# CIN tower: VectorE half a chunk behind TensorE, layer 0's K-tiles in the slots where pairs close, the first small product on VectorE

## What is computed

```python
e = stack([tbl_f[ids[:, f]] for f in range(32)], axis=1)     # 512 x 32 fields x 32
def cin(x0, filters):                                        # two layers, fp32
    prev, outs = x0, []
    for W in filters:                                        # (1, 32*32, 128), (1, 32*128, 128)
        z = einsum('bhd,bmd->bhmd', x0, prev).reshape(b, h * m, d)
        prev = relu(einsum('bpd,pn->bnd', z, W[0]))
        outs.append(prev)
    return sum(concatenate(outs, axis=1), axis=-1)
h = concatenate([cin(e, (filter_0, filter_1)), dense_ctx], axis=1)
y = relu(relu(h @ W_top1 + b_top1) @ W_top2 + b_top2) @ W_top3
```

## Time and profile before

| | |
|---|---|
| median of the runs | 988.39 us (988.18 to 989.77, 3 runs) |
| the profiled execution | 989.2 us, its span 987.4 us |
| TensorE busy | 872.2 us (88%), 3444 matmuls |
| VectorE busy | 770.8 us (78%) |
| ScalarE busy | 646.3 us (65%) |
| GpSimd busy | 682.4 us (69%) |
| granted TensorE clock, mean | 0.988 |

### The profile page before, as it was taken

The page is one execution under the profiler, slowest core; times in us unless marked ns, Lnnn a source line. Parts: engine busy times, 40 slices in busy tenths (PEclk is TensorE's granted clock), DMA queues, the critical chain, the costliest instruction groups (busy, mean ns, idle before and its releaser), DMA issues.

```text
span 987.4 us, 13153 instructions
## 1 busy us (share of the span) xinstructions
PE 872.2 (88%) x3444; PEld 646.5 (65%) x3444; DVE 770.8 (78%) x2506; ACT 646.3 (65%) x2174; POOL 682.4 (69%) x460
## 2 busy tenths in 40 slices
PE   0328999999999999999999999999999999999967
PEld 0105777776777777776777777776777777777743
DVE  0112888987888888898888888888888888888892
ACT  1208776777776777677777677777777767776702
POOL 6776887776787778777787777665666666666610
PEclk9998999999999999999999999999999999999988
DMA  9043221212222222212122222212111112110000
GB/s 255 14 147 114 73 72 59 62 60 72 72 72 72 72 73 72 64 59 67 62 72 73 73 72 72 71 59 87 47 50 70 70 69 70 70 59 1 1 1 0
DMA packets 34670, 66.64 MB, mean 67 GB/s; under 512 B 6226, under 2 KB 19762, under 8 KB 30403
## 3 DMA queue, kind: packets, MB, share of 16 engines
q1 hardware_dynamic: 27570, 59.94, 17.7%
q0 software_dynamic: 4096, 2.11, 1.8%
q10 hardware_dynamic: 2928, 3.76, 1.3%
HBM read 62.64 MB, written 5.24 MB: 69 GB/s over the span
## 4 chain that ended last, share of the span: by engine, by line
PE 66%; DVE 24%; POOL 5%; issue 3%; ACT 1%; DMA 0%; POOLq 0%
DVE acc L503 12%; PE acc L578 11%; PE yd L560 10%; PE yd L562 9%; PE yd L561 9%; PE ya L560 8%; PE ya L562 8%; PE ya L561 8%; POOL emb L260 5%; DVE yd L512 5%; DVE prev_lo L474 2%; DVE yd L503 2%; DVE sum L485 2%; DVE sum L518 1%; ACT scaled L399 1%
## 5 line engine op out<-in xcount | busy, mean ns | idle before, releaser
L399 ACT ACTIVATE scaled<-ya,emb 128x128 f32<-128x128 f32 x2048 | 584.2, 371 | 236.9 <-PE ya L562 234.7
L503 DVE SCALAR_TENSOR_TENSOR acc<-yd,emb,acc 128x128 f32<-128x128 f32 x1792 | 484.9, 341 | 105.1 <-PE yd L562 105.1
L279 POOL TENSOR_TENSOR half<-scaled 128x1024 f32<-128x1024 f32 x128 | 306.3, 2393 | 206.2 <-ACT scaled L399 205.1
L560 PE MATMUL yd<-w_hi,prev_hi 128*128 128x512 f32 x512 | 242.1, 473 | 44.1 <-DVE sum L518 43.3
L560 PE MATMUL ya<-w_hi,prev_hi 128*128 128x512 f32 x512 | 202.4, 395 | 3.5 <-ACT scaled L399 1.8
L561 PE MATMUL yd<-w_lo,prev_hi 128*128 128x512 f32 x512 | 202.1, 395 | 0.0
L562 PE MATMUL yd<-w_hi,prev_lo 128*128 128x512 f32 x512 | 201.9, 394 | 0.0
L561 PE MATMUL ya<-w_lo,prev_hi 128*128 128x512 f32 x512 | 200.9, 392 | 0.0
L562 PE MATMUL ya<-w_hi,prev_lo 128*128 128x512 f32 x512 | 200.9, 392 | 0.0
L283 POOL TENSOR_TENSOR part<-half 128x512 f32<-128x512 f32 x128 | 165.1, 1290 | 18.1 <-POOL half L279 0.4
L560 PEld LDWEIGHTS yd<-w_hi,prev_hi 128*128 128x128 f32 x512 | 97.1, 190 | 103.0 <-DVE sum L518 63.6
(11 more groups left out here) (52 smaller groups left out, 365.8 us busy)
## 6 DMA issues: line engine op xcount, KB each, us to landing
xb<-xt_scratch SPq DMA_DIRECT2D x32, 1024.0 KB, 5.0
x<-xt_scratch SPq DMA_DIRECT2D x64, 192.0 KB
xm<-xt_scratch SPq DMA_DIRECT2D x32, 256.0 KB, 4.8
emb<-in_tbl,idx POOLq DMA_INDIRECT x128, 2.5
scaled<-in_L_rec_filter SPq DMA_DIRECT2D x8, 256.0 KB, 6.1
xt_scratch<-xt_stage SPq DMA_DIRECT2D x7, 256.0 KB
xt_scratch<-xt_stage SPq DMA_DIRECT2D x9, 128.0 KB, 1.9
w_second_index_twice<-in_L_rec_filter ACTq DMA_DIRECT2D x2, 512.0 KB, 6.0
```

Source lines behind the costliest of these rows:

```text
L279: pool.tensor_tensor(half[:], piece[:, 0:AB * C // 2], piece[:, AB * C // 2:AB * C], ALU.add).then_inc(halved, 1)
L399: op = act.activation(scaled[:, tile % PR, C * j + N * i:C * j + N * (i + 1)], ya[:, n % RA, N * i:N * (i + 1)], ACT.Copy, scale=scale_of( ...
L503: dve.scalar_tensor_tensor(after, y_part, scale_of(c, q, HB * j + i), before, ALU.mult, ALU.add).then_inc(chained, 1)
L560: pe.matmul(dst, v_hi, m_hi, start=start, stop=False)
```

## The change

- D banks trail by half a chunk: slots 0 to 3 hold pair 1 of chunk c-1, slots 4 to 7 pair 0 of chunk c itself. The last round has four slots.
- K-tiles: slots 2 and 3 hold K-tiles 2 and 3 of chunk c+1 and the rest, slots 6 and 7 K-tiles 0 and 1 of chunk c+2. VectorE's products stand in slots 0 and 1 and in 5 and 6. `whole` has three buffers (`WH`).
- prev_high, prev_low and the addition to sum0 move to slot 4, copy_xm to slot 2, small_high (of chunk c+2) to slot 7; on GpSimd small_product (of chunk c+2) stands behind the tile sum of q = 1, small_low at the chunk's beginning.
- A pair's first instruction no longer adds part; `finish_pair` has four additions, and waits for part there.
- Chunk 0's small product and its low part are made by VectorE; `TURN_LEAD` is 3, `EARLY_NEXT` 22; xb is loaded in two halves.

```diff
@@ SyncE
+            def load_l0(c):
+                load_xm(c)
+                load_xb(c, 0)
+                load_x16(c)
+                load_xb(c, 1)
@@ GpSimd
-            small_product(0)
-            small_low(0)
+            small_product(1)
             for c in range(CHUNKS):
                 if c + 1 < CHUNKS:
-                    small_product(c + 1)
+                    small_low(c + 1)
                 for q in range(DC):
                     sum_tile(c, q)
...
-                    if q == 0 and c + 1 < CHUNKS:
-                        small_low(c + 1)
+                    if q == 1 and c + 2 < CHUNKS:
+                        small_product(c + 2)
                     if q == 1 and c % CPB == CPB - 1:
                         fold0(c // CPB)
@@ ScalarE
             copy_xm(1)
+            small_high(1)
...
-                        if j % 2 == 0 and c + 1 < CHUNKS:
-                            if s == 2:
-                                small_high(c + 1)
-                            if s == 6:
-                                prev_high(c + 1)
-                    if s == 5 and c + 2 < CHUNKS:
+                        if j % 2 == 0 and s == 4 and c + 1 < CHUNKS:
+                            prev_high(c + 1)
+                    if s == 2 and c + 2 < CHUNKS:
                         copy_xm(c + 2)
+                    if s == 7 and c + 2 < CHUNKS:
+                        small_high(c + 2)
@@ VectorE
+            def first_small():
+                dve.wait_ge(x16_loaded, 32)
+                dve.tensor_tensor(small[:], x16[:, 0, :], x16[:, 1, :], ALU.mult).then_inc(small_ready, 1)
+                dve.wait_ge(small_hi_ready, 1)
+                low_third = small_split[0:F]
+                dve.tensor_tensor(low_third, small[0:F], low_third.bitcast(F32), ALU.subtract).then_inc(small_lo_ready, 1)
...
+                            dve.tensor_scalar(after, y_part, x, None, ALU.mult).then_inc(chained, 1)
...
-                for k in range(1, HB):
+                dve.wait_ge(part_ready, DC * c + 2 * pair + 2)
+                for k in range(HB):
...
-                for s in range(SLOTS):
-                    if c > 0:
-                        add_banks(c - 1, s // 4, s % 4)
-                    if c + 1 < CHUNKS and s < KT:
-                        product(c + 1, s)
-                    if c > 0 and s % 4 == 3:
-                        finish_pair(c - 1, s // 4)
-                    if s == 6 and c + 1 < CHUNKS:
+                for s in range(SLOTS if c < CHUNKS else SLOTS // 2):
+                    at, pair = (c - 1, 1) if s < 4 else (c, 0)
+                    if at >= 0:
+                        add_banks(at, pair, s % 4)
+                    if s < 2 and c + 1 < CHUNKS:
+                        product(c + 1, 2 + s)
+                    if s in (5, 6) and c + 2 < CHUNKS:
+                        product(c + 2, s - 5)
+                    if s % 4 == 3 and at >= 0:
+                        finish_pair(at, pair)
+                    if s == 4 and c + 1 < CHUNKS:
                         prev_low(c + 1)
                         add_to_sum0(c + 1)
@@ TensorE
+                    at, pair = (c - 1, 1) if s < 4 else (c, 0)
                     for j in (2 * (s % 2), 2 * (s % 2) + 1):
-                        if c > 0:
-                            bank_d(c - 1, 2 * (s // 4) + j % 2, s % 4)
+                        if at >= 0:
+                            bank_d(at, 2 * pair + j % 2, s % 4)
...
-                    if c + 1 < CHUNKS:
-                        if 2 <= s < 2 + KT:
-                            layer0(c + 1, s - 2)
-                        if s == 1 + KT:
+                    if (s in (2, 3) and c + 1 < CHUNKS) or (s in (0, 1) and c == 0):
+                        layer0(c + 1, s)
+                        if s == 3:
                             layer0_rest(c + 1)
+                    if s in (6, 7) and c + 2 < CHUNKS:
+                        layer0(c + 2, s - 6)
```

More of the change, by code:

```diff
@@ L41, in cin_tower @@
     PR = 3
+    WH = 3
     EARLY = 3 * F // 4
-    EARLY_NEXT = 20
+    EARLY_NEXT = 22
     GATHER_CHUNKS = 20
@@ L77, in cin_tower @@
         x16 = sb("x16", [3 * F, 2, C])
-        whole = sb("whole", [P, 2, C])
+        whole = sb("whole", [P, WH, C])
         small = sb("small", [3 * F, C])
@@ L133, in cin_tower @@
         xm_loaded = sem("xm_loaded")
-        xb_loaded = sem("xb_loaded")
+        xb_loaded = [sem(f"xb_loaded_{r}") for r in range(2)]
         x16_loaded = sem("x16_loaded")
@@ L165, in cin_tower @@
         y_written = sem("y_written")
-        TURN_LEAD, TURN_SLOT = 2, 2
+        TURN_LEAD, TURN_SLOT = 3, 2
         def turns_before(c):
@@ L182, in turn_number @@
             return 0 if bt == 0 else turns_before(c) + AB * DC * c + 2 * TURN_SLOT
-        PAIR_STEPS = 2 * HB * DB + HB - 1
+        PAIR_STEPS = 2 * HB * DB + HB
         def d_number(c, q, j):
@@ L231, in load_l0 @@
                 for s in range(2):
-                    sp.dma_start(x16[:, s, :], dram(xt, at + 16 * C * s, [[0, 3], [C, F], [1, C]])).then_inc(
+                    sp.dma_start(x16[:, s, :], dram(xt, c * CH + 16 * C * s, [[0, 3], [C, F], [1, C]])).then_inc(
                         x16_loaded, 16)
+            def load_l0(c):
[3 more added lines that the diff above has]
+                load_xb(c, 1)
             sp.wait_ge(a_used, 1)
@@ L466, in product @@
                     dve.wait_ge(xm_in_psum, c + 1)
[L467 to L470, removed]
+                if k % 2 == 0:
+                    dve.wait_ge(xb_loaded[k // 2], 16 * (c + 1))
+                if n >= WH:
+                    dve.wait_ge(whole_used, n - WH + 1)
+                dve.tensor_tensor(whole[:, n % WH, :], xb[:, k, :], xm_ps[:], ALU.mult).then_inc(product_ready, 1)
             def prev_low(c):
@@ L490, in add_banks @@
                 dve.wait_ge(d_ready, n + 2)
-                if j == 0:
-                    dve.wait_ge(part_ready, DC * c + 2 * pair + 2)
                 for i in range(HB):
@@ L495, in add_banks @@
                         q, slot = 2 * pair + t, (n + t) % RD
-                        y_part = yd[:, slot, N * i:N * (i + 1)]
-                        before = part[:, c % 2, q, 0, :] if i == j == 0 else acc[:, t, :]
+                        y_part, x = yd[:, slot, N * i:N * (i + 1)], scale_of(c, q, HB * j + i)
                         after = y_part if (j, i) == (DB - 1, HB - 1) else acc[:, t, :]
-                        if (i, j) != (0, 0):
+                        if (i, j) == (0, 0):
+                            if g > 0:
+                                dve.wait_ge(chained, PAIR_STEPS * g)
+                            dve.tensor_scalar(after, y_part, x, None, ALU.mult).then_inc(chained, 1)
+                        else:
                             dve.wait_ge(chained, chain_count(g, j, i, t) - 2)
[L501 to L504, removed]
+                            dve.scalar_tensor_tensor(after, y_part, x, acc[:, t, :], ALU.mult, ALU.add).then_inc(chained, 1)
             def finish_pair(c, pair):
@@ L518, in finish_pair @@
                     dve.scalar_tensor_tensor(sum1[:, bt], total, 0.0, sum1[:, bt], ALU.max, ALU.add).then_inc(summed1, 1)
-            for k in range(KT):
+            for k in range(WH):
                 product(0, k)
+            first_small()
+            product(0, WH)
             prev_low(0)
             add_to_sum0(0)
+            product(1, 0)
+            product(1, 1)
             for c in range(CHUNKS + 1):
-                for s in range(SLOTS):
-                    if c > 0:
-                        add_banks(c - 1, s // 4, s % 4)
-                    if c + 1 < CHUNKS and s < KT:
-                        product(c + 1, s)
-                    if c > 0 and s % 4 == 3:
-                        finish_pair(c - 1, s // 4)
-                    if s == 6 and c + 1 < CHUNKS:
+                for s in range(SLOTS if c < CHUNKS else SLOTS // 2):
[9 more added lines that the diff above has]
+                    if s == 4 and c + 1 < CHUNKS:
                         prev_low(c + 1)
@@ L577, in layer0 @@
                 pe.wait_ge(product_ready, n + 1)
-                pe.matmul(acc0[:], w0[:, k, :], whole[:, n % 2, :], start=k == 0, stop=False).then_inc(whole_used, 1)
+                pe.matmul(acc0[:], w0[:, k, :], whole[:, n % WH, :], start=k == 0, stop=False).then_inc(whole_used, 1)
             def layer0_rest(c):
```

15 lines of the change are left out of this document (8 added, 7 removed).

## The result

The changed kernel takes 991.63 us (median of 17 runs, 989.99 to 992.82), the kernel before beside it 989.42. The ratio is 1.0023, 95% interval 1.0016 to 1.0030. Forecast were 979.1 and a range of 966 to 986. The profiled execution of the changed kernel took 992.44, its span 990.4.

What follows compares the result with a forecast made beforehand. Bound: TensorE with one stall behind VectorE. D banks from 85.0, 29 chunks of 26.97 (782.1), turns 5.7, folds 4.6 and the end put VectorE's loop end at 955.7, 9.3 saved: 979.1 us, range 966 to 986.

Steps and rivals of the forecast that it cites:

- What bounds the kernel: Steady loop: TensorE with one stall behind VectorE, 1.27 us idle in a chunk's second slot; prev_low and sum0 delay the close.
- The places of the new waits: TensorE waits at slots 5, 6 and 7 of each chunk: 0.21, 0.35 and 0.46 us, each with a 0.10 restart.
- The release, T + 6.83: From T, a closing slot's first matmul, TensorE is released after 2.28 + 2.20 + 4 x 0.467 + 0.48 = 6.83 us.
- The fourth addition: Part's first quarter, added at each pair's close on VectorE, adds 0.467 us to each close.
- Rival (d): Nothing to measure: waits 0.1 us longer at each of three places per chunk, 987.8 us; chance 0.06.
- The plain multiply: VectorE's multiply by a scalar, replacing the multiply-add with part, taken as 0.26 us as now: no saving that can be shown.
- The folds: At c = 7, 15 and 23 sum0 waits for GpSimd's half sum: 1.85 us twice and 0.9, 4.6 in all.
- The start: Chunk 0: ScalarE begins at 74.6 and D banks at 85.0, 10.95 us sooner.
- Port contention: At the start, first_small's two VectorE instructions amid GpSimd's gathers cost 0 to 1.4 us; 0.5 taken.
- (a): Product in time for slot 6, so that wait and its restart go: 26.52 us a chunk, 966 us; chance 0.12.
- (b): TensorE stops waiting at all in the loop: 25.6 us a chunk, about 939 us; chance 0.03.
- (c): Three gaps a chunk bring TensorE's clock down to its 1.2 GHz level: about 1049 us; chance 0.05.

Runs made afterwards that it cites:

- early-wait run: Changed kernel with VectorE's wait for part moved from between closing multiply-adds and additions to ahead of the last two banks: 992.39 us, ratio 1.0034.
- whole lag: Changed kernel, D banks a whole chunk behind again, part as third operand, three additions: 968.55 us; with product and fold sooner 948.29; with small_high(1) later too 943.70.
- small_high run: Changed kernel with ScalarE's small_high(1) behind the two banks of chunk 0's first slot instead of ahead of them: 986.6 us, ratio 0.9965.
- product run: Changed kernel with the product for slot 6's K-tile ahead of slot 5's multiply-adds on VectorE: 975.0 us, ratio 0.9860.
- fold run: Changed kernel with GpSimd folding sum0 ahead of the tile sum of q = 1: 986.55 us, ratio 0.9976.

## Why the forecast was wrong

**What bounds the kernel: right.** The old stall was sum0 and prev_low ahead of the closing banks; moving sum0 alone gave 18 us.

**The places of the new waits: right. Their sizes: each a little too small, and this is the greater part of the miss.** "One stall of 1.27 is traded for three" is what the timeline shows. But two terms of the sum were mis-sized, and they are the step that failed in the loop.
- The release, T + 6.83, came at T + 6.91 (T is 414.43, that is 413.57 and 0.86; TensorE goes on at 421.34). Closing multiply-adds to first addition take 2.27 (416.72 to 418.99) and not 2.20: the wait for part now stands between two instructions that depend on each other. The early-wait run shows the 0.07, and that most of it can't be had back by moving the wait to that place. The forecast put the wait instruction itself at nothing; what it waits for is long there (the pair that closes at 432.85 had its part at 422.47).
- The product was seen 0.83 after its start (426.53 to 427.36), not 0.73.

Put into the same recurrence these give: K-tile at 12.93, slot 7 at 13.89, release at 20.80, next T3 at 27.23, measured 27.21. 0.24 a chunk is small against 26.97, but the forecast gain was only 0.18, 0.7% of a chunk. Rival (d), 0.1 at each of three waits, is the nearest for the loop: 0.30 a chunk, and it had 6 in 100. The range's edge allowed 0.07 at each, 0.21, and that was too little, because every error of size goes through the three waits one after another (0.08, 0.10, 0.08). Its 987.8 has the start as forecast; the 3.7 us missing there make up most of the rest. By its own signs the forecast is wrong twice: the pitch is over 27.2 (27.21), and the start is off by more than 1.5.

**The plain multiply: right.** "The first saves nothing that I can show" holds: 341 ns on average for the multiply as for the multiply-add that took part in the kernel before, 342 for the other multiply-adds.

**The fourth addition: right in size, not weighed.** It was in the sum at 2 x 0.47. What the sum didn't ask is what the half lag costs against the same change without it. With measured sizes TensorE arrives at a closing bank at T + 6.62 or T + 6.37; three additions release it at 6.44 (at 6.37 without the wait for part in between), four at 6.91. So three just fit and four never do, and every chunk pays 1.0. By the runs the half lag itself costs little or nothing in the loop: between the changed kernel (27.21) and the whole lag with the same places (26.11) lie 1.10, of which 0.95 are the fourth addition. The other 0.15 fit the two waits for part of 0.07, which the whole lag has elsewhere; no run takes out these alone.

**The folds: right.** Their chunks were longer by 1.72 at c = 7, by 1.76 at c = 15 in the small_high run, and by 0.9 at c = 23, against 1.85 twice and 0.9. The changed kernel's profiled execution had 3.34 at c = 15, and the 1.6 more are the clock, which the sum had at nothing. TensorE waits 2.03 for `whole` in both fold chunks, but only after the second do matmuls follow each other at 0.43 instead of 0.23, which is the 1.2 GHz level:

```profile
291.28 1.10 PE L601 MATMUL acc<-whole,w 128*128 128x512 f32 x2 [2.03 <-DVE whole L480]
...
292.91 0.40 PE L583 MATMUL ya<-w_hi,prev_hi 128*128 128x512 f32 x1
293.14 0.39 PE L584 MATMUL ya<-w_lo,prev_hi 128*128 128x512 f32 x1
```
```profile
512.65 1.66 PE L601 MATMUL acc<-whole,w 128*128 128x512 f32 x2 [2.03 <-DVE whole L480]
...
514.53 0.63 PE L584 MATMUL yd<-w_lo,prev_hi 128*128 128x512 f32 x1
514.96 0.63 PE L585 MATMUL yd<-w_hi,prev_lo 128*128 128x512 f32 x1
```

**The start: half right.** D banks came 7.2 us sooner, where 10.95 was forecast. The step that failed is "VectorE, whose products start at 58.50, releases it near 62". The small product stands behind the third product, which waits for the second half of xb; and SyncE issues that half last. The chain of waits there, in order:

```profile
54.27 11.88 DMA xb<-xt_scratch
66.17 0.69 DVE whole L480
66.86 0.61 DVE small L499
67.49 0.72 SPq L237
68.20 0.04 issue
68.25 8.70 DMA x<-xt_scratch
76.95 0.07 issue
77.02 1.26 POOL small L306
78.31 0.63 ACT small_split L394
78.94 1.02 ACT scaled L408 x4
```

From VectorE's release at 67.49 to the landing at 76.95 it took 9.5, where the forecast had 8.7 from the earlier trace rows; the release was 5.5 us late, and this is the greater part. ScalarE's first bank came at 78.84 and not at 74.6, and the D banks followed. The forecast had read SyncE's new order and followed only x16 through it, although it was the change's own split of xb that put half of it behind x16. And the load in one piece shows that the order was not the whole of it: chunk 0's x16 itself lands 12 us after its issue. What can be had is ScalarE's order: small_high(1) behind the first banks gives 3.1.

**Port contention: not seen.** The gathers at 66.66 and 67.91, beside VectorE's small (66.78) and small_split (68.16), had their usual 0.94 and 0.30, though both instructions have two operands in SBUF. The 0.5 for it was not needed.

**The rivals.** (a) did not come in the changed kernel. The product run brings it about: without the product's wait the pitch is 26.69, where the text had 26.52; the difference is the two releases, 2 x 0.08. (b), 25.6, needed both closes below 6.5: with three additions and the product in time it is 25.71, in the whole lag. (c), frequent short idle times bringing the clock down, didn't: no fall shows at the three recurring waits, and a chunk without a fold or a turn lasts 27.17 to 27.24 throughout. The Trainium skill, "TensorE: Matmul & The Clock Gate", section "A second HAM failure mode: psum-queue depth-cycling", spoke for (c). This case's traces don't agree for gaps of 0.3 to 0.5, three a chunk; they show falls after some single gaps of 2.0 and none after others.

## What to carry to other kernels

A wait instruction is not free because what it waits for is long there: where a loop is released by a chain of dependent instructions, count each instruction and each wait in that chain, and ask first at what time the other engine arrives. A lag of half a tile has to be paid with whatever it takes out of an existing operand; here 8.6 us once against 1.0 in every one of 31 chunks. A forecast gain of 0.7% of a pitch has no sign yet, where two of the sizes that the pitch is built from can be off by 0.07 and 0.10. And where a change splits a load, follow both halves through the new order.

## What the runs showed of the hardware that I had not expected

- The same idle time of TensorE, 2.03 us in the same code, is followed by the lower clock in some executions and places and not in others. It fell at c = 15 but not at c = 7 in the changed kernel, at both in the early-wait run, at neither in the small_high run and in the run with xb in one piece; in the fold run the gap itself is gone. Gaps of 2.4 to 2.5 do the same: a fall at both in the whole lag, at c = 15 alone without the fourth addition (30.17 against 28.53). Where it fell, the chunk took 1.6 us more. The granted clock over equal stretches of the changed kernel, around c = 7 and c = 15 (it stands behind POOL's count):

```profile
285.00:300.00 15.00, 12.62 (x51) 9.13 (x50) 12.41 (x40) 9.63 (x33) 11.24 (x9) 1.00 0.16 50
505.00:520.00 15.00, 12.97 (x46) 9.38 (x47) 10.93 (x37) 8.44 (x30) 9.61 (x9) 0.89 0.15 41
```

- A wait between two dependent instructions of VectorE adds 0.07 us even when what it waits for is long there; ahead of an instruction that waits anyway a second one adds 0.05 (closing multiply-adds start 0.43 after the last D matmul's start, 0.48 to 0.49 in both runs with the early wait).
- Loads at the start land late, the small ones too: the two of x16, 192 KB each, were there 8.7 us after the second was issued (68.25 to 76.95), and 12 us after the first was issued at 52.91. The halves of xb, 512 KB, took 8.7 us in the middle between 52 and 80, and 3.8 over the whole span. The gathers run there, and so do the other loads; no run tells their shares apart.
